# A gated recurrence as 121 chunks of 17 tokens where it was 86 of 24, with its state copies on ScalarE and its bias split on GpSimd

## What is computed

```
states = A_pow[None] * jnp.cumsum(B_all / A_safe[None], axis=1)
ssm_out = jnp.einsum('bsn,dn->bsd', states, C_w) + C_b
def step(h, xt):
    cat = jnp.concatenate([xt, h], axis=-1)
    ff1 = jnp.tanh(cat @ ff1_w.T + ff1_b)
    ff2 = jnp.tanh(cat @ ff2_w.T + ff2_b)
    t_i = jax.nn.sigmoid((cat @ ta_w.T + ta_b) * TIME_DELTA + (cat @ tb_w.T + tb_b))
    h_new = ff1 * (1.0 - t_i) + t_i * ff2
    return (h_new, h_new)
layer_out = x + cfc_out @ out_w.T + out_b
```

## Time and profile before

| what | us |
|---|---|
| median of 3 runs (1546.15 to 1547.73) | 1547.21 |
| the profiled execution, its own time | 1546.65 |
| its span, slowest core (core 2) | 1545.0 |
| spans of the 8 cores | 1532.2 to 1545.0 |
| busy: TensorE, VectorE, ScalarE, GpSimd | 1240.5, 1096.4, 908.4, 771.6 |

### The profile page before, as it was taken

One profiled execution on the slowest core, in us unless ns is written; L12 is line 12 of the kernel. 1 busy time (PEld: TensorE's weight loads), 2 busy tenths in 40 slices (PEclk: granted clock), 3 DMA queues, 4 the chain that ended last, 5 costly groups with the idle time before them and its releaser, 6 DMA issues. The chain is left out here.

```text
span 1545.0 us, 32324 instructions; the slowest of 8 cores (1532.2 to 1545.0 us)
## 1 busy us (share of the span) xinstructions
PE 1240.5 (80%) x10500; PEld 841.0 (54%) x10500; DVE 1096.4 (71%) x2130; ACT 908.4 (59%) x1335; POOL 771.6 (50%) x718
## 2 busy tenths in 40 slices
PE   1124655899999999999458886668899999998998
PEld 0013433566666666665247774455566666665644
DVE  4699797788788788773635555587787887877740
ACT  2446866677787877773123331566676766766641
POOL 1266189586686775676600344025363553633531
PEclk9976766999999999999779998798999999999999
DMA  8816444212222212115030001010111211111011
GB/s 276 285 55 218 163 164 177 62 42 56 70 69 56 56 62 51 42 56 150 25 86 3 3 3 56 28 55 18 66 69 70 83 39 72 56 42 42 28 55 55
DMA packets 40684, 118.38 MB, mean 77 GB/s; under 512 B 4388, under 2 KB 12740, under 8 KB 40520
## 3 DMA queue, kind: packets, MB, share of 16 engines
q1 hardware_dynamic: 29144, 107.10, 19.8%
q0 software_dynamic: 11376, 9.22, 3.8%
HBM read 97.17 MB, written 25.70 MB: 80 GB/s over the span
## 5 line engine op out<-in xcount | busy, mean ns | idle before, releaser
L822 PE MATMUL bank<-xqT,w1q 128*128 128x258 bf16 (+1 forms) x4352 | 583.6, 281 | 99.5 <-DVE y L1170 52.6
L822 PEld LDWEIGHTS bank<-xqT,w1q 128*128 128x128 fp8e4 x4352 | 427.7, 102 | 258.6 <-issue 119.2
L851 PE MATMUL bank<-w2q,q 128*128 128x512 fp8e4 x2112 | 531.5, 381 | 0.0
L1397 POOL TENSOR_TENSOR y<-y,Rb 128x1024 f32<-128x1024 f32 (+1 forms) x136 | 338.1, 2509 | 200.8 <-ACT Rb L1042 200.8
L1002 ACT ACTIVATE y<-bank,convbs,convws 128x256 f32<-128x256 f32 (+1 forms) x544 | 295.6, 553 | 166.8 <-PE bank L822 154.9
L1228 DVE SCALAR_TENSOR_TENSOR y<-bank,convws,y 128x256 f32<-128x256 f32 (+1 forms) x544 | 256.0, 471 | 193.3 <-ACT y L1002 192.0
L851 PEld LDWEIGHTS bank<-w2q,q 128*128 128x128 f16 x2112 | 205.0, 98 | 165.2 <-issue 6.3
L1170 DVE SCALAR_TENSOR_TENSOR y<-bank,convws,y 128x256 f32<-128x256 f32 (+1 forms) x544 | 253.5, 466 | 0.1
L939 ACT ACTIVATE y<-y 128x1024 f32<-128x1024 f32 (+1 forms) x136 | 140.0, 1029 | 115.3 <-DVE y L1170 113.4
L1111 DVE TENSOR_TENSOR M<-M,ab 128x1024 f32<-128x1024 f32 (+1 forms) x119 | 195.8, 1645 | 1.9 <-ACT ab L951 1.9
L961 ACT ACTIVATE q<-y,qoff 128x1024 f16<-128x1024 f32 (+1 forms) x136 | 151.2, 1114 | 22.9 <-POOL y L1397 12.9
(11 more groups left out here) (200 smaller groups left out, 1458.9 us busy)
## 6 DMA issues: line engine op xcount, KB each, us to landing
w2r<-w2T SPq DMA_DIRECT2D x28, 1024.0 KB, 6.7
w1r<-w1T SPq DMA_DIRECT2D x7, 2048.0 KB, 25.7
x1t<-xall SPq DMA_DIRECT2D x19, 512.0 KB, 3.6
basebuf<-x1t SPq DMA_DIRECT2D x17, 512.0 KB, 2.6
xg<-xall SPq DMA_DIRECT2D x16, 512.0 KB, 4.6
x1t<-x2buf SPq DMA_DIRECT2D x16, 512.0 KB, 3.6
out<-x1t SPq DMA_DIRECT2D x16, 512.0 KB, 2.6
xg<-basebuf SPq DMA_DIRECT2D x14, 512.0 KB, 4.2
```

What stands on the lines that cost most here:

```text
L822: mm = pe.matmul(a_bank(n)[:, 0:tw + 2], w1q[:, c, k * P:(k + 1) * P], xqT[j % 3][:, c, 0:tw + 2], start=c == 0, stop=c == DC - 1)
L851: pe.matmul(pB[e % 2][:], q[:, qs, kh, :], w2q[:, kh, 512 * h:512 * h + 512], start=kh == 0, stop=False)
L1397: pool.tensor_tensor(v, v, Rb[:, 0:w].unsqueeze(1).to_broadcast([P, 4, w]), ALU.mult).then_inc(scaled_done, 1)
```

## The change

CN becomes 121 and CL 17, so a core has 17 + 17 = 34 steps on 121 columns. The gate and mix buffers get wider; mixd and mixu move to another part of memory. The copy of a step's hidden state into hC is made by ScalarE, behind the four gates of the next step, and for the last step behind its own. The split of the bias is issued by GpSimd right behind the loads, with the same five operations and waits. The waits of VectorE for hc_done stay.

```diff
@@ -33,8 +33,8 @@
 T = 256
 NG1, NG2 = 18, 17
 NT1, NT2 = 9, 8
-CN = 86
-CL = 24
+CN = 121
+CL = 17
 CW = 17
 SJC = CN + 1
 ROUND_SLOT = {16: 0, 18: 1, 20: 2, 23: 3, 25: 4, 27: 5, 30: 6}
@@ -170,14 +170,14 @@
     st_ = at('states', YB + 16384 + 8704, [P, WLEN + 16])
     sJ = at('sJ', YB + 16384 + 8704 + 8768, [P, CL, SJC], BF16)
     GB = YB + 16384 + 8704 + 8768 + 4192
-    gateF = [at(f'gateF{i}', GB + i * 1376, [P, 2, 2, CN]) for i in range(2)]
-    gateT = [at(f'gateT{i}', GB + 2752 + i * 704, [P, 2, CN]) for i in range(2)]
-    mixd = [at(f'mixd{i}', GB + 4160 + i * 704, [P, 2, CN]) for i in range(2)]
-    mixu = [at(f'mixu{i}', GB + 5568 + i * 704, [P, 2, CN]) for i in range(2)]
-    pick = at('pick', GB + 6976, [P, 12, CN], BF16)
-    bpad = at('bpad', GB + 9056, [P, P])
-    bT = at('bT', GB + 9568, [P, P], BF16)
-    assert GB + 9824 <= YB + YR * T * 4
+    gateF = [at(f'gateF{i}', GB + i * 1952, [P, 2, 2, CN]) for i in range(2)]
+    gateT = [at(f'gateT{i}', GB + 3904 + i * 992, [P, 2, CN]) for i in range(2)]
+    mixd = [at(f'mixd{i}', XQT + 4096 + i * 992, [P, 2, CN]) for i in range(2)]
+    mixu = [at(f'mixu{i}', XQT + 6080 + i * 992, [P, 2, CN]) for i in range(2)]
+    pick = at('pick', GB + 5888, [P, 12, CN], BF16)
+    bpad = at('bpad', GB + 8800, [P, P])
+    bT = at('bT', GB + 9312, [P, P], BF16)
+    assert GB + 9568 <= YB + YR * T * 4
     hcur = [at(f'hcur{j}', MB + j * 1376, [P, KC, CN], BF16) for j in range(2)]
 
     def small(name, cols, dt=F32):
@@ -1572,10 +1572,15 @@
         pool.dma_start(ow[:], owT.rearrange('(k p) d -> p k d', p=P)).then_inc(ow_in, 16)
         pool.dma_start(ob32[0:1, :], obr).then_inc(ob_in, 16)
         pool.dma_start(ob32[32:33, :], obr).then_inc(ob_in, 16)
-        hv = hC[:].rearrange('p b (c k) -> p b c k', k=CL)
-        for s in range(CW, NSTEP):
-            pool.wait_ge(h_done, 2 * s + 2)
-            pool.tensor_copy(hv[:, :, :, s - CW], hcur[s % 2][:]).then_inc(hc_done, 1)
+        pool.memset(obhl[:], 0.0).then_inc(ob_split, 1)
+        pool.wait_ge(ob_split, 1)
+        pool.wait_ge(ob_in, 32)
+        pool.tensor_copy(obhl[0:1, :], ob32[0:1, :])
+        pool.tensor_copy(obhl[32:33, :], ob32[32:33, :]).then_inc(ob_split, 1)
+        pool.wait_ge(ob_split, 2)
+        pool.tensor_tensor(ob32[32:33, :], ob32[32:33, :], obhl[32:33, :], ALU.subtract).then_inc(ob_split, 1)
+        pool.wait_ge(ob_split, 3)
+        pool.tensor_copy(obhl[32:33, :], ob32[32:33, :]).then_inc(ob_split, 1)
 
 
 
@@ -1617,6 +1622,12 @@
                     mm.then_inc(gate_mm, 1)
 
     def cfc_act():
+        hv = hC[:].rearrange('p b (c k) -> p b c k', k=CL)
+
+        def keep_h(s):
+            act.wait_ge(h_done, 2 * s + 2)
+            act.activation(hv[:, :, :, s - CW], hcur[s % 2][:], AF.Identity).then_inc(hc_done, 1)
+
         for s in range(NSTEP):
             gb = bank[4 * (s % 2):4 * (s % 2) + 4]
             for half in range(2):
@@ -1627,11 +1638,12 @@
                 act.wait_ge(gate_mm, 4 * s + 2 * half + 2)
                 act.activation(gateT[half][:].rearrange('p b c -> p (b c)'), gb[2 * half + 1][:, 0:2 * CN], AF.Tanh,
                                scale=0.5).then_inc(gate_done, 1)
+            if s > CW:
+                keep_h(s - 1)
+        keep_h(NSTEP - 1)
 
     def cfc_dve():
         for s in range(NSTEP):
-            if s == 1:
-                bias_dve()
             for half in range(2):
                 n = 2 * s + half
                 f1, f2, tt = gateF[half][:, 0], gateF[half][:, 1], gateT[half][:]
@@ -1650,17 +1662,6 @@
                     dve.tensor_scalar(hh[:, :, 0:1], hh[:, :, 0:1], pcs[:, 4:5], None, ALU.mult).then_inc(h_done, 1)
                 else:
                     dve.scalar_tensor_tensor(hh, mixu[half][:], 0.5, f1, ALU.mult, ALU.add).then_inc(h_done, 1)
-
-    def bias_dve():
-        dve.memset(obhl[:], 0.0).then_inc(ob_split, 1)
-        dve.wait_ge(ob_split, 1)
-        dve.wait_ge(ob_in, 32)
-        dve.tensor_copy(obhl[0:1, :], ob32[0:1, :])
-        dve.tensor_copy(obhl[32:33, :], ob32[32:33, :]).then_inc(ob_split, 1)
-        dve.wait_ge(ob_split, 2)
-        dve.tensor_tensor(ob32[32:33, :], ob32[32:33, :], obhl[32:33, :], ALU.subtract).then_inc(ob_split, 1)
-        dve.wait_ge(ob_split, 3)
-        dve.tensor_copy(obhl[32:33, :], ob32[32:33, :]).then_inc(ob_split, 1)
 
 
     setup_sp()
```

## The result

The changed kernel takes 1533.39 us (median of 4 runs, 1532.46 to 1534.31) against 1547.19; the ratio is 0.9916, 95% interval 0.9904 to 0.9929. That is 13.8 us less. The forecast was 17.6 less, 1529.6, with a range to 1534.5: the time lies in the range, at its upper end. Executions in which the cores of one die had a lower granted clock and the time was longer (1554.85 us of split_pool_gaps and 1606.64 of best among them) are left out of every time given here. The profiled execution, 1534.31 us with a span of 1532.8, was slowest on core 7.

What follows compares the result with a forecast made beforehand. The recurrence's cycle of six VectorE instructions, eight L1616 matmuls and one activation was taken as the bound, not TensorE. Terms -18.4 + 0.9 - 0.5 + 0.45 = -17.6 us gave 1529.6 against the median, range 1525.8 to 1534.5.

Steps and rivals of the forecast that it cites:

- The stall: Step 1 to 2 of the recurrence: VectorE's wait for the output bias, 13.6 us all on the path, goes.
- Fewer, wider steps: Recurrence: 41 steps become 34, 4.31 us early and 4.45 late; first-to-last gate, stall included, -18.4 us.
- own bounds: Whole kernel: 1527 to 1533 us, from matmul pace, last copy's price, pick hidden and VectorE growth; forecast's chance 82%.
- rival 3: First steps run badly beside output-weight load and GpSimd's split: something like +4 to +8, 1533.6 to 1537.6 us; chance 7%.
- signs named for being wrong: Recurrence: period above 4.6 us, TensorE's groups following without idle time, or first ten steps longer than the next.
- What becomes late next is nothing: Bias split on GpSimd: bias wanted only 150 us later, split ends by 815 us, nothing queued behind; no cost.
- The copies on ScalarE: Hidden-state copies behind each step's last gate: 0.58 us each, fitting 3.0 us free; end of recurrence -0.5 us.
- the other bound: End of the recurrence: +1.4 us if ScalarE's last copy cost GpSimd's price, 2.48 us, instead of 0.58.
- pick and the joints: Before the recurrence: pick grows to 1452 elements, +0.45 us on the path (between 0 and 0.5); sJ copies unchanged.
- step 0: First step of the recurrence: the same growth as other steps with its first matmuls at half clock, +0.9 us.
- Rivals: 1 and 2: Recurrence: TensorE becomes the bound, 1616 us, chance 3%; ScalarE reloads its table before gates, +20.5, 1550 us, chance 2%.
- Rival 4: Start of project_out: full clock outlives the shorter pause, first matmuls save about 3 us, 1526.6 us; chance 6%.

Runs made afterwards that it cites:

- split_pool_gaps: Changed kernel with the bias split still on GpSimd, its four late instructions timed behind VectorE's last instruction of steps 7, 9, 11, 13; 1529.4 us (one run).
- best: split_dve_gaps with VectorE's hc_done wait ahead of its mixu wait and the last copies shared between GpSimd and ScalarE; 1525.55 us (3 runs), ratio to before 0.9866.
- before_split_gaps: Kernel before the change with only the bias split moved, one VectorE instruction per step behind the last hcur of steps 7 to 11; 1533.71 us, ratio 0.9913.
- split_dve_gaps: Changed kernel with the bias split back on VectorE, one instruction per step behind the last hcur of steps 7 to 11; 1529.57 us, ratio to before 0.9887.
- copies_on_pool: split_dve_gaps with the hidden-state copies back on GpSimd at 121 columns; 1532.5 us (one run).
- copy_contig: split_dve_gaps with ScalarE's copies to contiguous places of hC instead of 34 bytes apart, so project_out treats permuted tokens; 1526.9 us (one run).

## Why the prediction was right, and where it was off

The direction held, and so did the mechanism of the two large terms, the stall and the wider steps. The size held less well. The forecast's own bounds were 1527 to 1533; 1533.39 is above them, and inside the range only because that took in the lower half of rival 3. It is luck that the start came out 0.85 us better than forecast, against +3.6 for the split and +1.5 for the end. One of the signs named for being wrong came true in part: one of the first ten steps is longer than the next, 7.92 us against 4.32. The parts of the sum:

- *The stall* was worth 13.6 us by the rows, and before_split_gaps gave 13.5 in all. Right.
- *Fewer, wider steps.* 4.31 and 4.45 us a step by three slopes; measured 4.32 and 4.45. TensorE stayed off the path with 54 ns a matmul, the margin of 0.06 us included. The sum of 141.7 for the gates came out in split_dve_gaps to the tenth. Against 146.7 of before_split_gaps the wider chunks bring 5.0 us there.
- *What becomes late next is nothing*, of the split on GpSimd: this is the step that failed. It looked at who waits for GpSimd's result, and not at what GpSimd's instructions keep from VectorE. They cost 3.6 us on core 7. I had weighed the rule on the shared port pair (the Trainium skill, SBUF — State Buffer, "SBUF: two separate sides") and put it aside because the earlier trace rows showed a mixd unharmed beside a copy. One row was not enough: that copy had been running for 1.15 us when mixd came, and by copies_on_pool only its first part holds. The rule is right here in that VectorE's instructions with two SBUF inputs are blocked by GpSimd instructions that read SBUF, and that a memset does not block them; "for the whole instruction" held for the casts and the subtraction, and not for the strided copy, 1.5 of 2.27 us. Rival 3 had the mechanism, with the right lower bound of 2.7 us, at 7%. The trace of the kernel before had a second sign, in the other direction, which I did not look for (timeline of core 2):

```profile
758.63 4.47 DVE L1551 TENSOR_TENSOR_SCAN states<-acol,carry,wt 128x2048 f32<-128x2048 f32 x1
758.98 4.63 POOL L1378 TENSOR_TENSOR mrk<-mve,chalf 128x2 f32<-128x2 f32 x1
```

A GpSimd instruction on 2 elements, 0.73 us in the median of its 17 executions, lasts 4.63 us there, until 0.5 us after the end of VectorE's scan.
- *The copies on ScalarE.* "I take 0.58, as ScalarE's writes of bf16 have this rate": mis-sized, 2.31. The row it came from wrote contiguously. That it is hidden in all steps but the last held, though wider gates made ScalarE busy for 1.58 us a step, not 1.42 (18.65 us from 809 to 860, 11.8 steps); the other bound, +1.4 at the end by GpSimd's price, was near the truth: the end went from 5.30 to 6.32, +1.0 where I had -0.5. "GpSimd's own copies cost the path nothing before but the last" held at 86 columns; at 121 they would have cost 0.13 a step.
- *pick and the joints*, +0.45 with +0.9 for step 0: too much. In the timeline of the changed kernel pick has its 1.67 us, but the copy of sJ, 1938 elements from places 68 bytes apart, takes 1.95 where 1944 from 96 bytes apart took 2.55, and GpSimd's small instruction beside it 1.58 where it took 2.38:

```profile
743.30 1.67 DVE L1531 TENSOR_TENSOR pick<-idb 128x1452 bf16<-128x1452 bf16 x1
...
764.93 1.95 DVE L1556 CAST sJ<-states 128x1938 bf16<-128x1938 f32 x1
...
765.16 1.58 POOL L1380 TENSOR_TENSOR mtm<-mrk 128x2 f32<-128x2 f32 x1
```

From the start of VectorE's statistics instruction ahead of `ssm_begin` (L1163) to the first gateF of step 1 it was 46.0 us before (735.92 to 781.90, core 2) and is 46.4 now (737.03 to 783.47, core 7): +0.5 in place of +1.35.

Rivals: 1 and 2 did not happen (54 ns; one table load). Rival 4 neither: project_out's first four matmuls took 1.86 us again. But a shorter pause can bring it about: in copy_contig, after 3.90 us of idle TensorE, core 7 began at full clock. My argument against it, that 3.18 us of idle had been enough for half clock elsewhere, did not carry over to this place.

The balance of core 7 against core 2 of before: gates -14.85 (forecast -18.4), start +0.5 (+1.35), end +1.0 (-0.5), together -13.4. The first pass, up to L1163, took 1.1 us more (735.92 and 737.03), which gives the -12.3 between the two profiled executions; the difference of the medians is -13.8.

## What to carry to other kernels

An idle engine is no free place for work if what it reads from SBUF holds the engine that bounds the step. Idle time inside the bounding engine's own list, here 1.5 us behind the last instruction of each step, can be free where the idle engine is not. Take the price of a copy from a row with the same spacing of what it writes, not only the same count and type; and of two waits ahead of an instruction, put the one that was met long ago first.

## What was not expected of the hardware

- A GpSimd instruction that reads SBUF held VectorE's instructions with two SBUF inputs: 0.41 us became 1.05 beside a cast of 1024 elements in one partition, and up to 2.16 beside a subtraction of 2.11. One partition was enough. Beside a memset of 1024 elements there was no effect.
- A copy of 484 bf16 elements to places 34 bytes apart takes 2.31 us on ScalarE and 2.27 on GpSimd, nearly the same; to contiguous places ScalarE takes 0.63. On GpSimd it held VectorE for about the first 1.5 us only (copies_on_pool).
- The order of two waits is worth 0.05 to 0.07 us on the path of each instruction. In the late steps of the changed kernel hcur starts 0.58 to 0.59 behind mixu (which started at 925.51 and 926.94), with the wait for hc_done met long before. From the timeline of core 7:

```profile
925.75 2.33 ACT L1629 ACTIVATE hC<-hcur 128x484 bf16<-128x484 bf16 x1
...
926.10 0.41 DVE L1664 SCALAR_TENSOR_TENSOR hcur<-mixu,gateF 128x242 bf16<-128x242 f32 x1 [0.17 <-DVE mixu L1655]
...
927.52 0.41 DVE L1664 SCALAR_TENSOR_TENSOR hcur<-mixu,gateF 128x242 bf16<-128x242 f32 x1 [0.17 <-DVE mixu L1655]
```

In best it is 0.53, with both waits still there, so it is their order and not their number. The first of these three lines is the copy that runs beside it, on ScalarE, without effect on VectorE.
